# VectorE's order in the attention rounds: a count moved from ahead of a round's masks to behind its sums

## The reference

```
h = x_flat @ W_gat                      # (nodes, 4 heads, 4 experts)
src, dst = edge_index (524288 edges) + one loop a node
e = leaky_relu(a_src[src] + a_dst[dst])
ee = exp(e - segment_max(e, dst)[dst])
denom = segment_sum(ee, dst)
agg = segment_sum(h[src] * ee / denom[dst], dst) + b_gat
scores = layernorm(agg) averaged over heads; the best 2 of 4 experts, softmax
out = sum over experts of gate * (gelu(x @ W1 + b1) @ W2 + b2)
```

## Time and profile before

| | us |
|---|---|
| median of 3 runs (lowest, highest) | 4058.1 (4051.01, 4058.19) |
| span of the profiled execution | 4750.1 |
| its rounds, from the first gathers to the third block | 2376.5 to 4593.2 |

### The profile page before, as it was taken

The page is one execution under the profiler, slowest core; times in us unless marked ns, Lnnn a source line. Parts: engine busy times, 40 slices in busy tenths (PEclk is TensorE's granted clock), DMA queues, the critical chain, the costliest instruction groups (busy, mean ns, idle before and its releaser), DMA issues. The chain is left out here.

```text
span 4750.1 us, 30403 instructions
## 1 busy us (share of the span) xinstructions
PE 2949.0 (62%) x8964; PEld 1485.1 (31%) x8964; DVE 3244.3 (68%) x5382; ACT 1526.0 (32%) x2234; POOL 1184.2 (25%) x1252
## 2 busy tenths in 40 slices
PE   6987889999989998866603444334433443345207
PEld 3433333444434443334401222222222222122107
DVE  7899688888887988776445555555544555557587
ACT  2331254444544544455301222212211112112107
POOL 0000000000000000111175445444445555554400
PEclk9989989999999999977756666666566666667559
DMA  4113224544545463856511111111101111011127
GB/s 168 62 58 122 79 72 128 176 147 143 183 123 183 157 209 125 267 185 214 143 17 23 31 31 31 31 31 31 31 22 31 25 31 32 23 14 13 32 109 275
DMA packets 336048, 452.11 MB, mean 95 GB/s; under 512 B 80429, under 2 KB 251832, under 8 KB 326922
## 3 DMA queue, kind: packets, MB, share of 16 engines
q1 hardware_dynamic: 289722, 390.77, 25.2%
q0 software_dynamic: 46160, 59.39, 5.5%
HBM read 340.18 MB, written 109.85 MB: 95 GB/s over the span
## 5 line engine op out<-in xcount | busy, mean ns | idle before, releaser
L1554 POOL DMA_INDIRECT got<-scratch_tab,src_at x1120 | 1065.1, 951 | 341.3 <-issue 341.3
L1508 PE MATMUL hid_ps<-tokens,w 128*128 128x512 f32 x512 | 336.6, 793 | 1068.5 <-ACT hid L1832 580.1
L699 PE MATMUL in_ps<-tokens,w_in 128*128 128x512 f32 x2048 | 939.8, 611 | 24.5 <-ACT zst L906 19.8
L699 PEld LDWEIGHTS in_ps<-tokens,w_in 128*128 128x128 f32 x2048 | 394.8, 197 | 507.6 <-issue 507.6
L1508 PEld LDWEIGHTS hid_ps<-tokens,w 128*128 128x128 f32 x512 | 114.2, 247 | 1192.8 <-ACT hid L1832 604.7
L716 PE MATMUL out_ps<-w_out,act 128*128 128x512 f32 x1024 | 475.7, 608 | 3.9 <-DMA w_out<-in_m_WoutT 3.9
L626 POOL MEMSET tokens<- 1x128 int32 x1 | 0.2, 195 | 1905.6 <-DVE tokens L1098 1905.6
L1097 DVE TENSOR_TENSOR tokens<-tokens 128x1024 f32<-128x1024 f32 x380 | 465.2, 1224 | 11.2 <-ACT tokens L864 10.2
L1524 PE MATMUL y_ps<-w,hid 128*128 128x128 f32 x2048 | 331.0, 314 | 225.5 <-issue 222.0
L1098 DVE TENSOR_TENSOR tokens<-tokens 128x1024 f32<-128x1024 f32 x380 | 464.9, 1224 | 0.0
L1824 ACT ACTIVATE ys<-y_ps 128x512 f32<-128x512 f32 x128 | 76.5, 597 | 1156.5 <-remote 819.5
(11 more groups left out here) (325 smaller groups left out, 4291.7 us busy)
## 6 DMA issues: line engine op xcount, KB each, us to landing
w_out<-in_m_WoutT SPq DMA_DIRECT2D x256, 512.0 KB, 4.5
w_in<-in_m_WinT SPq DMA_DIRECT2D x128, 512.0 KB, 3.9
scratch_y<-ys SPq DMA_DIRECT2D x25, 1024.0 KB
got<-scratch_tab,src_at POOLq DMA_INDIRECT x1120
tokens<-scratch_xt SPq DMA_DIRECT2D x8, 2048.0 KB, 10.0
scratch_sz<-zst SPq DMA_DIRECT2D x64, 256.0 KB, 4.6
gz<-scratch_sz SPq DMA_DIRECT2D x64, 256.0 KB, 4.7
ys<-scratch_y SPq DMA_DIRECT2D x9, 1024.0 KB, 11.6
```

Of the source, the lines that this page charges most:

```text
L699: last = t_.matmul(in_ps[:, z, :], w_in[:, n % WIN, k, :], xT[:, s % 2, k, :], start=(k == 0), stop=(k == KC - 1))
L1508: last = t.matmul(hid_ps[:, f], w1[:, e, f * P:(f + 1) * P], tokens[:, g * QW:(g + 1) * QW], start=True, stop=True)
L1554: g.indirect_dma_start(got[:, y, t, :], None, tab_d[:, :], bass.IndirectOffsetOnAxis(ap=src_at[:, y, t:t + 1], axis=0))\
```

## The change

In `pair` of VectorE the call of `count` goes from ahead of `compute` to behind it, in the written-out rounds and in the loop. The round thereby has the order merge, masks, wait for `by_value`, sums, count, where it had merge, count, masks, wait, sums. In the loop's code the wait for the last node's keys (`s_last`) stays ahead of `merge`. The `count` ahead of the first round stays where it is. No other engine's code is changed.

```diff
                                 v.sem_inc(s_rem, 1)
-                            count(ck, b_first[:, (r + y + 1) * FR:(r + y + 2) * FR])
                             if turn:
                                 loop_rounds(ck)
                         else:
                             v.wait_ge(s_last, 16 * (r + y + 1) - 16 * (2 * PAIRS - 1))
                             merge(ck, r + y + 1, 1 - y, FR, FD)
-                            count(ck, b_k[:, 1 - y])
                         compute(ck, y, FR if first else FD)
+                        count(ck, b_first[:, (r + y + 1) * FR:(r + y + 2) * FR] if first else b_k[:, 1 - y])
                     v.sem_clear(s_mch)
```

## The result

The changed kernel takes 4075.2 us, the median of 5 runs (4074.8 to 4080.2), against 4058.1 (also 5 runs, 4051.0 to 4060.0) before. The ratio is 1.0047, with a 95% interval of 1.0036 to 1.0058, so 14.6 to 23.5 us more; 20.4 was forecast.

The account below looks back on a forecast made before the run. GpSimd was taken to bound the timed kernel in the attention rounds, without the trace's stalls; 0 + 0 + 0 + 20.4 us on the median of 4058.1 gave 4078.5 us, range 4065 to 4090 (8 in 10: 4053 to 4110).

Parts of the forecast that it names:

- Step 1: First round: VectorE's wait for the first by_value grows from 11.1 to 31.5 us, so moving the count gains nothing.
- Step 2: Rounds between: VectorE's 73.0 us stay under GpSimd's 82.45; spare for the next indices falls from 45 to 24.6; cost 0.
- The forecast's check on the median: Sum of the kernel's path before the change, without the trace's stalls: 4036 us, 0.5% under the median.
- Step 3: Last two rounds, of 48 gathers: VectorE sets the pace and waits for nothing in either order; cost 0.
- Step 4: End of the rounds: the count behind the last sums has no cover, so its whole 20.4 us is added.
- The first rival: No loss: with gathers under 1.07 us, VectorE is late at the first by_value; 4058 to 4071 us, chance 0.17.
- The second: Rival, slower by far: the trace's stalls hold in timed runs, 17 counts join the chain; 347 us more, 4405, chance 0.11.
- The third: Rival, faster: last sums end 20.4 us earlier, their store and load run beside the count; 4051 us, chance 0.07.

## Why the prediction was right, and where it wasn't

The sum: 20.4 forecast, 17.1 by the medians (14.6 to 23.5), 20.5 between the by_value of round 15 and the third block of the two clean profiles. The two whole spans differ by more, 28.4; 8.7 of that lie between the first by_value and that of round 15 (1256.8 against 1248.1 us). Here is the first of these two in the changed kernel, and behind it a gather of 1.99 us:

```profile
2458.03 0.43 DVE L1705 TENSOR_TENSOR logit<-by_value,a_dst 128x256 f32<-128x256 f32 x1 [32.19 <-ACT by_value L1842]
...
3131.23 1.23 DVE L1715 TENSOR_TENSOR add<-by_value,add 128x1024 f32<-128x1024 f32 x1 [1.16 <-ACT add L1847]
3131.29 1.99 POOL L1554 DMA_INDIRECT got<-scratch_tab,src_at  x1 [0.30 <-issue]
```

Most of the 8.7 us is in the gathers: those of the written-out rounds are busy for 985.8 us in the one profile and 977.6 in the other. 14 of them take over 1.9 us in the one and 9 in the other, all of them begun 0.05 to 0.1 us behind the start of VectorE's product at L1715. Whether the order has a part in that stays open. From the first by_value to that of round 15 it is 1250.5 to 1256.8 us in the three profiles whose written-out rounds have their counts moved or left out, and 1243.5 to 1248.2 in the four clean ones with the counts ahead of the masks, so a few us may be the order's; but the gathers over 1.9 us number 7 to 14 and 4 to 9, which overlap. The interval of the change's runs leaves no more than 3 us for it.

Step 1, the first round: waits of 11.1 and 31.5 were worked out, 12.1 and 32.2 measured. Step 2, the rounds between: GpSimd's round was put at 82.45 and is 83.2 before and 83.8 after on average, VectorE's slack at 9 and is 8 to 11; no cost, and without the counts nothing is gained. The forecast's check on the median, 4036 us, came out 14 under the clean span for this reason in the main (15 rounds are 11.4 longer than 15 x 82.45), without a part in the difference that was forecast. Step 3: no wait in the last two rounds, in either order. Step 4: 20.37 more between the last sums and the third block.

The account of step 4 was right in its sum and too narrow in its reason. It said that the count at the end has no cover, and hung that on the last sums' ending where they ended. The runs show that this condition is the cause: with the end alone moved the last sums do end 20 us earlier, and the bare count costs 0.6 us there. What the change loses is the cover of the count of round 15, which stood ahead of the last wait and now stands behind it. The first rival's point was put at the first by_value for the same reason; it lies at the last one that has a wait, round 15, and that wait held (8.6 and 8.5 us in the two clean profiles).

The first rival needed gathers below 1.07 us: they are 0.955 + 0.305 = 1.26 in the clean profile of before, gaps included. The second needed the stalls in the timed runs: the clean profiles, as long as the runs, have none. The third needed a late load of the sums: it landed 28 us ahead of its first reader (3926.0).

One forecast failed outright: that the profiled span of the changed kernel would grow by some 300 us. It shrank by 672. The step that failed is the reading of the first profile as a recording that holds the engines back. Its consequence for the timed runs was right (they have no stalls), but seven other recordings with the same instructions or nearly so, one of them of the same kernel, show none either. So the rule of the Trainium skill on recording ("NOTIFIC — the notification-queue block", section 7.1) is neither borne out nor excluded as the cause in that one execution. By that section the inside of the recording block always holds its producers back; when the memory that takes the records is full, it depends on a setting whether the block holds back, drops the new record or overwrites an old one. No run here shows any of this at work, and what held the engines back in that execution stays open.

## What to carry to other kernels

Where one engine waits for another in each of many rounds, and the inputs of the engine that sets the pace still come in time (26 us were to spare here), a piece of work is free ahead of the last of these waits, as far as the wait is long enough, and costs its full length behind it. Find that wait and count what stands on either side of it. Moving work to the far side of a wait in every round shows up once, not once a round, since each wait but the last takes it back. And compare a profile's span with the timed median first: a profile that is 17% longer than the runs can have the wrong engine waiting in every round, while the durations of VectorE's instructions and of the gathers, and the sum made of them, still hold.

## What the runs showed of the hardware

An indirect DMA of 128 rows of 96 bytes takes GpSimd 944 to 947 ns at the median, with 0.30 us ahead of the next, in all eight profiles, the stalled one too, and whether VectorE counts beside it or waits. The exception is VectorE's product of 128 x 1024 at L1715 (1.23 us). In all eight profiles a gather that starts 0.05 us or more behind the product's start, while it runs, doesn't end before 0.81 us behind the product's end, and so takes up to 1.99 us; one that starts at most 0.04 us behind the product's start takes its 0.94. None of the gathers over 1.2 us falls on a count's instructions. Why the product holds a gather and a count doesn't wasn't tested.

The profiled execution of before with the stalls (span 4750.1) and the one without (4050.0) differ by 700 us at equal instructions. All of it lies in the attention rounds: the first gather starts at 2376.5 and 2375.2 us, and from the third block's start to the end it is 156.9 and 156.7 us. In the stretches read the earlier trace rows the other engines than GpSimd were held back in it, and only while gathers ran.
